# Four graph layers on one core: the last slots' eviction goes to VectorE, part of the search goes later, the measure of x goes ahead of the slots' turning

## The reference

```python
agg = segment_sum(x[src], dst)                   # the sum that every layer has
x = layernorm(x + relu(relu((x + agg) @ W1.T + b1) @ W2.T + b2))        # layer 0
x = layernorm(x + four_gcn_convolutions(x))                             # layer 1
x = layernorm(x + edge_feature_convolution(x, edge_attr_64))            # layer 2
x = layernorm(x + two_sage_convolutions(x))                             # layer 3
```

## Time and profile before

| | us |
|---|---|
| median of 3 executions | 2607.56 (2598.77 to 2608.9) |
| the profiled execution | 2607.76, span 2606.0 |
| busy in the span: PE / DVE / ACT | 2483.1 / 1323.9 / 611.8 |
| 50 to 75 us: PE / DVE / ACT busy | 14.48 / 22.21 / 17.76 of 25 |
| 75 to 100 us | 21.30 / 24.52 / 19.01 of 25 |
| 125 to 150 us | 21.37 / 23.23 / 20.74 of 25 |
| 300 to 325 us | 24.73 / 18.92 / 23.26 of 25 |

### The profile page before, as it was taken

How to read it: one execution, slowest core, us unless ns; L and a number is a source line. 1 busy time by engine, 2 the same in 40 slices (tenths; PEclk the granted TensorE clock), 3 DMA queues, 4 the chain that set the end, 5 groups by cost and what they waited for, 6 DMA issues and landing times.

```text
span 2606.0 us, 38625 instructions
## 1 busy us (share of the span) xinstructions
PE 2483.1 (95%) x15714; PEld 1466.2 (56%) x15714; DVE 1323.9 (51%) x3578; ACT 611.8 (23%) x742; POOL 168.1 (6%) x117
## 2 busy tenths in 40 slices
PE   1889999879999999999999999999999999999998
PEld 0778888744555555555555555555555555555545
DVE  6887777577887666676666333332222211222222
ACT  2889899650000111111111000000000000000000
POOL 4100000020000011111111000000000200000000
PEclk9999999989999999999999999999999999999999
DMA  5737222336777566666666565544544545445554
GB/s 161 90 99 74 101 98 98 151 92 201 228 234 221 174 189 183 190 182 181 188 187 186 148 189 142 140 137 137 138 138 128 146 138 140 137 135 156 150 151 113
DMA packets 292285, 395.37 MB, mean 152 GB/s; under 512 B 82216, under 2 KB 279076, under 8 KB 288644
## 3 DMA queue, kind: packets, MB, share of 16 engines
q1 hardware_dynamic: 241336, 326.08, 44.9%
q10 hardware_dynamic: 49964, 64.80, 7.9%
q0 software_dynamic: 800, 1.94, 0.2%
HBM read 343.43 MB, written 49.32 MB: 151 GB/s over the span
## 4 chain that ended last, share of the span: by engine, by line
PE 87%; DVE 4%; ACT 3%; DMA 2%; issue 1%; SPq 1%; DVEq 1%; POOL 1%; POOLq 0%; ACTq 0%
PE PS L1659 81%; PE PS L1842 1%; SPq L506 1%; DMA XN<-in_x_dram 1%; PE PS L1849 1%; PE PS L1850 1%; ACT HN L1445 1%; DMA HR<-adjacency 1%; PE PS L1864 1%; POOL AT L647 1%; DVE TB L935 1%; ACT HR L1445 0%; PE PS L1847 0%; PE PS L1846 0%; PE PS L1873 0%
## 5 line engine op out<-in xcount | busy, mean ns | idle before, releaser
L1659 PE MATMUL PS<-HR,HN 128*128 128x500 fp8e3 (+1 forms) x5096 | 1061.0, 366 | 4.8 <-DVE HN L1078 2.0
L1659 PE MATMUL PS<-HR,AGN 128*128 128x500 fp8e3 (+1 forms) x4606 | 918.8, 350 | 4.8 <-ACT HR L1445 2.1
L1659 PEld LDWEIGHTS PS<-HR,HN 128*128 128x128 f16 x5096 | 489.4, 97 | 522.5 <-issue 7.7
L1659 PEld LDWEIGHTS PS<-HR,AGN 128*128 128x128 f16 x4606 | 446.6, 97 | 402.8 <-ACT HR L1445 3.6
L1659 PE MATMUL PS<-TB 128*128 128x245 f16 x1250 | 321.3, 276 | 27.8 <-DVE TB L935 22.5
L935 DVE TENSOR_TENSOR TB<-S,HR 128x1240 f16<-128x1240 f16 x250 | 199.4, 797 | 0.0
L1155 DVE SCALAR_TENSOR_TENSOR AT<-PS,SC,TB 128x384 f32<-128x384 f32 (+24 forms) x50 | 21.6, 472 | 324.5 <-PE PS L1659 315.9
L935 DVE TENSOR_TENSOR TB<-iot,HN 128x640 f16<-128x640 f16 x250 | 122.4, 490 | 85.7 <-PE PS L1659 84.8
L1659 PEld LDWEIGHTS PS<-TB 128*128 128x128 f16 x1250 | 123.6, 100 | 53.1 <-DVE TB L935 19.7
L727 POOL TENSOR_TENSOR AT<-AT,dstI 128x1088 f32<-128x1088 f32 x49 | 100.3, 2047 | 763.8 <-DVE mxe L1280 763.8
L1513 ACT ACTIVATE SD<-VE 128x4 f32<-128x4 f32 (+1 forms) x39 | 8.0, 206 | 595.2 <-DVE VE L1200 595.2
(11 more groups left out here) (247 smaller groups left out, 1727.4 us busy)
## 6 DMA issues: line engine op xcount, KB each, us to landing
HR<-adjacency SPq DMA_DIRECT2D x588, 437.5 KB, 3.5
AT<-source_lanes ACTq DMA_DIRECT2D x49, 544.0 KB, 5.2
AT<-in_edge_attr_dram ACTq DMA_DIRECT2D x144, 128.0 KB, 3.1
adjacency<-HN SPq DMA_DIRECT2D x9, 1531.2 KB, 5.7
adjacency<-HR SPq DMA_DIRECT2D x8, 1531.2 KB, 5.5
adjacency<-TB SPq DMA_DIRECT2D x8, 1531.2 KB, 5.5
HR<-adjacency SPq DMA_DIRECT2D x49, 218.8 KB, 2.5
AT<-in_edge_attr_dram ACTq DMA_DIRECT2D x48, 160.0 KB, 4.1
```

The source lines that it names most:

```text
L1659: return t_.matmul(out_, w, m, start=start, stop=True, skip_group_check=True)
```

## The change

It has three parts, and no computation is added or left out. (1) Of each sub the 13th eviction group, its last two slots, goes from ACT to DVE (`last_windows`, new semaphore `s_ed`). (2) In the loop `find_edge` goes from slot 4 to slot 20, `decode` from slots 60 to 102 to slots 90 to 132, the turning of slots and weights to later slots. (3) Ahead of the loop PE's `measured_line` and DVE's `scale_of` go ahead of the slots' decoding and turning, and ACT makes three pieces of `HI[0]` ahead of its copy to `V4[0]`.

```diff
-        TURN_AT = {120: 2, 134: 4, 170: 6, 184: 8}
-        WEIGHT_AT = {220: (0, 4), 236: (4, 6)}
+        TURN_AT = {170: 2, 184: 4, 220: 6, 234: 8}
+        WEIGHT_AT = {270: (0, 4), 286: (4, 6)}
...
             measure_line(1)
-            for step in range(8):
-                decode(step, 0, WA)
             dve.wait_ge(s_c4, 1)
             scale_of(0, MS[:, P:P + 1])
             dve.drain().then_inc(s_scale, 1)
+            for step in range(8):
+                decode(step, 0, WA)
...
+            def last_windows(s):
+                if s >= 3:
+                    dve.wait_ge(s_aw[s % 3], 16 * (s // 3))
+                    dve.wait_ge(s_un, s - 2)
+                dve.wait_ge(s_cm, SUBW * (s + 1))
+                i0, i1 = EV[NEA]
+                b = 4 * ((NEV * s + NEA) % 3)
+                a3 = A16[s % 3].rearrange("p (h w d) -> p w h d", h=NB, d=WD)
+                v.tensor_scalar(a3[:, i0:i1, :, :], TW[:, b:b + i1 - i0, 0:HC].rearrange("p w (h d) -> p w h d", d=WD), UNIT, None, ALU.mult,
+                                saturate=False).then_inc(s_ed, 1)
+
             def diagonal(s):
-                dve.wait_ge(s_ev, NEV * (s + 1))
+                dve.wait_ge(s_ev, NEA * (s + 1))
+                dve.wait_ge(s_ed, s + 1)
...
             for t in range(NW):
+                if t % SUBW == 10 and t > SUBW:
+                    last_windows(t // SUBW - 1)
...
-                if t == 4:
+                if t == 20:
                     find_edge(WA, WG)
...
-                if t in range(60, 60 + 6 * 8, 6):
-                    decode((t - 60) // 6, WA, WG)
+                if t in range(90, 90 + 6 * 8, 6):
+                    decode((t - 90) // 6, WA, WG)
...
-                for k, (i0, i1) in enumerate(EV):
+                for k, (i0, i1) in enumerate(EV[:NEA]):
...
             measured_lane(1)
+            measured_line(1)
             pe.wait_ge(s_dec, 1)
...
-            measured_line(1)
             pe.wait_ge(s_ct, 1)
...
                         if i == LEAD:
-                            pe.wait_ge(s_ev, NEV * s)
+                            pe.wait_ge(s_ev, NEA * s)
+                            pe.wait_ge(s_ed, s)
```

More of the change, by code:

```diff
@@ L83, in build @@
     NEV = len(EV)
+    NEA = NEV - 1
     UNITS = [(2 * u, min(2 * u + 2, NS_)) for u in range(-(-NS_ // 2))]
@@ L338, in build @@
         s_un = sem("sub_summed")
+        s_ed = sem("last_windows_copied")
         s_dg = sem("nodes_themselves_counted")
@@ L988, in _ @@
                     v.tensor_scalar(flag[:, :], fs[:, 0:1], 0.5, None, ALU.is_gt).then_inc(s_flag, 1)
+            last_windows(NS_ - 1)
             diagonal(NS_ - 1)
@@ L1404, in _ @@
                 act.dma_start(flat_rows[o_:o_ + P * KJ].rearrange("(p j) -> p j", j=KJ), KP).then_inc(s_rows, 16)
-            act.wait_ge(s_ltp, 1)
-            c.copy(V4[0][:, 0:WA * P, :], PS[:, 0:WA * P].unsqueeze(2).to_broadcast([P, WA * P, REP])).then_inc(s_ct, 1)
             act.wait_ge(s_scale, 1)
             for q in range(NQ):
+                if q == 3:
+                    act.wait_ge(s_ltp, 1)
+                    c.copy(V4[0][:, 0:WA * P, :], PS[:, 0:WA * P].unsqueeze(2).to_broadcast([P, WA * P, REP])).then_inc(s_ct, 1)
                 cols = slice(q * QN, (q + 1) * QN)
@@ L1702, in _ @@
                     if t == 6 * SUBW:
+                        pe.wait_ge(s_wtc, 6)
                         pe.wait_ge(s_at, 4)
@@ L1733, in _ @@
                     if i % 4 == 0 and m >= 3:
-                        pe.wait_ge(s_ev, m - 2)
+                        s_, k_ = divmod(m - 3, NEV)
+                        if k_ < NEA:
+                            pe.wait_ge(s_ev, NEA * s_ + k_ + 1)
+                        else:
+                            pe.wait_ge(s_ed, s_ + 1)
                     h = SLOT * (t % (WB * RINGS))
@@ L1745, in _ @@
                                 pe.wait_ge(s_split, NQ)
[L1746 to L1749, removed]
+                            if s in (4, 5):
+                                pe.wait_ge(s_ct, 2 * s - 5)
                             if s == 7:
@@ L1756, in _ @@
                             done = k + 1
-            pe.wait_ge(s_ev, NEV * NS_)
+            pe.wait_ge(s_ev, NEA * NS_)
+            pe.wait_ge(s_ed, NS_)
             pe.wait_ge(s_at, NS_ - 2)
```

## The result

The changed kernel takes 2600.72 us (median of 20 executions, 2596.52 to 2604.02), the kernel before on the same chip 2605.23 (20 executions, 2598.77 to 2609.87). The ratio is 0.9982 with a 95% interval of 0.9976 to 0.9989: 4.5 us faster, by the interval 2.9 to 6.3. That is a change of less than 0.5%, and faster where the sum had said 0.8 us slower.

What follows compares the result with a forecast made beforehand. Limits by stage: the gather-to-store chain level with the loop, then DVE, then PE's waits for ACT at sub ends. Terms 6.3 + 0 + 1.3 + 0.6 - 7.0 - 0.4 = +0.8 on 2607.76 gave 2608.6 us, range 2596 to 2616.

Steps and rivals of the forecast that it cites:

- The search later: Gathers, index loads and first store: the later search delays the store, so ACT begins sub 3 at 119.3, +6.3 us.
- rival A: Chain not late: gathers issued freely at 1.25 us each, sub 3 begins 5.8 us sooner, 2596.5 us; chance 0.17.
- What the moved work frees becomes a wait: Before sub 3: decoding and copies freed in subs 1 and 2 turn into an ACT wait of some 12 us.
- Sub 3 at 0: Sub 3: ACT's shorter work and PE's slowness after the stop taken together as 0, bounds -0.5 and +2 us.
- subs 4 and 5 at +1.3: Subs 4 and 5, where DVE is the limit: two more evictions of 0.67 us each, +1.3 us.
- the flag at +0.6: Sub 6: PE also waits for the new eviction behind the one-hots, going on at about 171.7, +0.6 us.
- Ends of the steady subs: 17 ends of steady subs: about 0.41 of PE's 0.45 us wait goes at each, -7.0 us.
- rival B: Ends of subs gain nothing: ACT's twelfth group or DVE's eviction ends some tenths later; 2615.6 us, chance 0.12.
- The last end: After the last sub: the same PE wait as at the steady ends goes once more, -0.4 us.
- The new instruction: DVE's new eviction of each sub's last two slots: 0.67 us, with room for it in the steady subs.
- Rival C: DVE's eviction is slow: at 1.12 us the gain is gone, from 1.4 us over 0.5% slower; chance 0.06.
- D: Both shifts larger: gathers at their upper bound and PE slow after the stop, +3.5 + 2, 2614 us; chance 0.07.

Runs made afterwards that it cites:

- e5: Changed kernel with all seven pieces of the low half ahead of the search (slots 8 to 20); 2601.2 us (one execution).
- e2: Kernel before with only the search, the decoding and the turns later in the loop; 2603.54 us, ratio 1.0004.
- e6: Changed kernel with the 16 index loads behind the store of sub 0 in SP's queue; 2592.41 us, ratio 0.9958 to the kernel before.
- e11: Kernel before with only the store of sub 0 put ahead of the index loads; 2602.96 us against 2602.64, ratio 1.0001.
- e8: Changed kernel run once more for its profile, nothing changed; 2600.41 us (one execution).
- e9: e6 with the eviction of sub 5's last two slots ahead of the flag's work on DVE; 2590.83 us, ratio 0.9955 to the kernel before.
- e12: Changed kernel timed again, nothing changed; 2597.55 us against 2602.64 for the kernel before, ratio 0.9981.
- e3: Kernel before with only the measure of x ahead of the slots' turning; 2601.17 us, ratio 0.9997.
- e7: Kernel before run once more for its profile, nothing changed; 2602.88 us (one execution).
- e10: e6 with the last eviction group of each sub left on ACT; 2597.87 us against 2602.64 for the kernel before, ratio 0.998.

## Why the prediction was right or wrong

**The search later, +6.3: wrong, about -0.3.** The step that failed is "then come four bare pairs until 71.15, the sixth gather is let through by the new eviction there". From the gathers of before, the one of 5.22 us above all, I had made a rule that only a change of instruction lets a gather through; but those that fitted it had nearly all begun at the same instant of a pair, and e5 shows five passing without such a change. That put the index loads 5.3 us too late (80.5 against 75.22), and the landing, 6.3 us in place of 7.67, put ACT another 1.4 too late. The Trainium skill, page "SBUF — State Buffer", section "Who interferes with whom", infers that `tensor_tensor` does not hold up descriptor generation; the traces here disagree with that too, since the same gather takes 1.21 us or 5.22 beside it. The truth lies between rule and forecast: the eight took 14.9 us, where the one said 10 and the other 20 or more. My rival A rested on free gathers and is not what happened either; it needed the chain 12 us sooner.

**What the moved work frees becomes a wait: right**, with half the size (6.45 us of 12). e2 (freed, no gain), e6 (the wait removed, 6 us gained by the marks) and e11 (nothing to gain in before) show it together.

**Sub 3 at 0, subs 4 and 5 at +1.3, the flag at +0.6: right in kind, too small.** Sub 3 costs 0.6 (0.35 late at its end, though begun 0.3 sooner), inside its bounds. From sub 3 to sub 7 it is +2.8, where my terms make 1.5 (1.3 + 0.6 less one end). Sub 4 takes +1.0 (21.2 against 20.1) where I had 0.65. Subs 5 and 6, with the flag between them, take +1.8 (42.0 against 40.1) where I had 0.65 + 0.6: I let PE go on 0.6 behind the one-hots, but DVE also stood 0.44 us for a DMA, and in e8 the lower clock behind the stop lasted longer than in the other two profiles of the changed kernel, without which it would be +1.4. Sub 7 comes out even, where I had one end's gain, because its time hangs on the clock (below). Spells at the lower clock so make some 0.7 of the 2.8 (below); whether the change has a part in them is open. e9 gives about 0.6 us back by order alone.

**Ends of the steady subs, -7.0: right mechanism, size -5.1.** The three ends do meet within 0.3 us (307.97 for ACT's twelfth group, 308.17 for the eviction, 308.27 for PE), rival B is excluded, and 0.30 us goes at each of 17 ends. I took 0.45 from the weight load's wait and 0.41 of it as gain. PE's own row says 0.27. The weight load's idle time has an ordinary gap in it: in the changed kernel, where PE waits for nothing at 308.27, the weight load is still idle for 0.13 us. The last end, sized at -0.4, is one of the same 0.30.

**The new instruction: right.** 0.69 us as a rule and 0.67 to 0.73 over all profiles; in the steady sub DVE is idle ahead of it. Rival C is excluded, D as well.

**The sum.** Term by term -0.3 + 0.6 + 2.8 - 5.1 is -2.0, and the ledger -1.9. The errors went against each other: 6.6 us too much for the search, 3.8 too little in the other terms. That the sum was only 2.8 us off by the ledger is partly luck. The medians say -4.5 (-2.9 to -6.3), e12 the same. The remaining 2.5 us are, in these five profiles, the stop near 260 us: it cost the two of before 3.7 us in the mean and the three of after 0.8, and behind the loop their means agree to 0.1 us (all profiles lie between 2114.1 and 2118.8 there). But only one profile of 14 has the long stop, so it need not stand behind the medians too. What does is not settled; spells at the lower clock and the part behind the loop vary by as much. The parts apart (-2.1, +1.0, -0.8 by the ratios) add up to -1.9, as the ledger does.

## What to carry to other kernels

Ahead of a wait for a transfer, freed time is worth nothing until one has looked at what stands in front of that transfer in its queue: 16 loads that nobody needed yet turned 6 us of gain into idle time, and moving one store in front of them brought it back. Size a wait from the idle time of the instruction that does the work, not from its weight load. Instances of a transfer that all meet a busy engine at the same instant are no rule, however many they are: vary what runs beside it, and when, before a sum rests on it. And a difference between two profiles is no gain until the same stretch has been compared between two executions of one kernel.

## What the runs showed of the hardware

**The clock falls at short stops.** Pairs of matmuls that take 0.38 us take 0.62 after some of PE's waits, and the granted clock of those stretches is the lower level, 1.2 of 2.4 GHz. In the changed kernel, windows over the stop at the store and that at the flag:

```profile
112.00:114.00 2.00, 0.00 (x0) 0.00 (x0) 0.00 (x0) 1.18 (x2) 0.00 (x0) 0.59 1.03 435
114.00:118.00 4.00, 3.92 (x20) 2.86 (x21) 1.21 (x2) 3.58 (x5) 0.00 (x0) 0.50 1.00 420
...
174.60:177.30 2.70, 2.70 (x14) 1.98 (x15) 2.63 (x6) 0.65 (x1) 0.00 (x0) 0.52 0.03 9
177.30:180.00 2.70, 2.70 (x28) 2.48 (x27) 2.70 (x8) 2.67 (x4) 0.00 (x0) 1.00 0.34 145
```

Ahead of them PE had waited 4.89 and 3.49 us. A long stop is not needed, and a shorter one does not always do it. The waits at the flag, 1.45 and 0.84 us in before and e3 alike, were followed by a granted clock of 0.58 in before (172 to 176 us) and of 1.00 in e3, whose sub 3 to sub 7 took 75.50 us, the least of all. Behind the wait of 2.2 us at the end of sub 6, from 186 to 198 us, the clock was 1.00 in before, e3 and e9 and 0.86 in e7, e6 and the changed kernel. Sub 7 then took 16.14 in before against 17.81 in e7, which is the 1.6 us by which these two profiles of one kernel differ (76.46 and 78.03); in e9 and e6, both with the new eviction, it took 15.85 and 17.52. From 58 to 66 us the clock was 0.50 in the changed kernel, and 1.00 in the mean of 50 to 75 in before; there PE waits for DVE, and it cost nothing that the marks show.

**A stop that no wait explains.** Around the stop of 3.66 us in before, two transfers on the instruction queue, of 8 KB each and begun at 257.6, took 4.39 and 3.80 us; the median of this size was 0.47 in the first 500 us of that profile. That they caused the stop is not shown: in e10 two such transfers begun near 252.4 took 4.14 and 2.86 us and PE did not stop, and e6 has a stop of 0.93 us without any that took over 2.4.
